# Window attention: the read-out R summed by 32x64 matmuls straight from the stored M, without spread copies

## The reference, cut to what matters

```
x = x + L0(gn(x))   # two GELU layers per pixel, 4 multipliers
x = x + L1(gn(x))   # 4x4 FIR filter
x = x + L2(gn(x))   # window attention
x = x + L3(gn(x))   # per-pixel 3x3 kernels, scatter-add, batch norm, leaky ReLU
```

```
q, k = split(x @ W_qk.T + b_qk)              # 4*64 query channels, 32 key channels
attn[c, d] = sum over the 64 pixels p of a window of q[c, p] * k[d, p]   # for each head
out = attn * temperature, laid out so that the 64 query channels c become the 64 pixels of the window
```

## Time and profile before

| what | us |
|---|---|
| median of 3 runs | 1149.85 |
| lowest, highest | 1148.54, 1150.21 |
| span of the profiled execution | 1148.0 |
| what lies around the span, if the profiled execution took the median | 1.85 |
| stage 4, first half of the images | 334.7 to 409.8 of the span |
| stage 4, second half | 832.2 to 906.4 |

### The profile page before, as it was taken

How to read it: one execution, slowest core, us unless ns; L and a number is a source line. 1 busy time by engine, 2 the same in 40 slices (tenths; PEclk the granted TensorE clock), 3 DMA queues, 4 the chain that set the end, 5 groups by cost and what they waited for, 6 DMA issues and landing times. The chain is left out here.

```text
span 1148.0 us, 22784 instructions
## 1 busy us (share of the span) xinstructions
PE 952.7 (83%) x6876; PEld 650.8 (57%) x6876; DVE 867.1 (76%) x1211; ACT 693.3 (60%) x860; POOL 317.6 (28%) x265
## 2 busy tenths in 40 slices
PE   5699977979989977845999949799999788676774
PEld 4333327968878875334433349688778683233332
DVE  7477788877757944876687878877769646799796
ACT  5799972323358853547999923234388563366564
POOL 0000009400026720510000066000077403466565
PEclk9799998989989988987999979989999898899897
DMA  9100000000000010233000000000000200024334
GB/s 294 37 0 0 0 0 1 0 1 1 0 1 1 0 73 5 69 114 107 0 0 0 0 1 1 1 1 0 1 1 0 74 0 1 0 86 135 106 114 146
DMA packets 51301, 39.32 MB, mean 34 GB/s; under 512 B 1600, under 2 KB 50880, under 8 KB 51008
## 3 DMA queue, kind: packets, MB, share of 16 engines
q1 hardware_dynamic: 51264, 38.85, 10.7%
HBM read 22.07 MB, written 16.78 MB: 34 GB/s over the span
## 5 line engine op out<-in xcount | busy, mean ns | idle before, releaser
L337 PE MATMUL ps<-work,cst 128*128 128x512 f32 x512 | 237.0, 610 | 17.5 <-ACT work L557 13.7
L337 PEld LDWEIGHTS ps<-work,cst 128*128 128x128 f32 x512 | 94.5, 193 | 158.8 <-issue 144.4
L256 PE MATMUL ps<-ST,work 128*128 x256 | 131.1, 635 | 9.7 <-DVE work L897 7.1
L557 ACT ACTIVATE work<-X,l0s 128x2048 f32 x64 | 136.6, 2140 | 2.6 <-SPq L294 2.6
L564 ACT ACTIVATE work<-ps 128x2048 f32<-128x2048 f32 x64 | 123.1, 1923 | 8.2 <-PE ps L337 8.0
L1019 POOL TENSOR_TENSOR work<-cst,ksum 128x512 f32<-128x512 f32 x64 | 66.2, 1055 | 203.2 <-SPq L294 174.4
L806 DVE TENSOR_TENSOR work<-ps,cst 64x512 f32<-64x512 f32 x128 | 88.2, 689 | 39.1 <-PE ps L404 37.3
L984 POOL TENSOR_TENSOR co<-mv,cst 128x1 f32<-128x1 f32 x8 | 1.5, 191 | 392.1 <-DVEq L246 302.4
L450 PE MATMUL ps<-work,cst 128*64 128x128 f32 x1024 | 103.6, 287 | 6.7 <-ACT work L621 6.7
L586 ACT ACTIVATE work<-ps 128x512 f32<-128x512 f32 x80 | 47.8, 598 | 100.5 <-PE ps L357 100.5
L450 PEld LDWEIGHTS ps<-work,cst 128*64 128x64 f32 x1024 | 88.4, 141 | 18.7 <-issue 9.9
(11 more groups left out here) (99 smaller groups left out, 1774.3 us busy)
## 6 DMA issues: line engine op xcount, KB each, us to landing
work<-x SPq DMA_DIRECT2D x32, 512.0 KB, 4.9
out<-work SPq DMA_DIRECT2D x64, 256.0 KB, 2.8
work<-choose SPq DMA_DIRECT2D x2, 2048.0 KB, 8.4
cst<-consts SPq DMA_DIRECT2D x1, 1009.5 KB, 9.6
cst<-consts SPq DMA_DIRECT2D x1, 64.0 KB, 2.0
```

Source lines behind the costliest of these rows:

```text
L256: return nc.tensor.matmul(ps[:, bank, :], sel[:, n, :], ST[:, ds(s * (4 * H), 4 * H)], start=True, stop=True)
L337: last = pe.matmul(ps[:, 4 * (m % 2) + b, :], wg[:, m, :], yb[:, m, b * BANK:(b + 1) * BANK], start=True, stop=True)
L557: act.activation(yb[:, m, :], X[:, ds(s * PIX + i * CHUNK, CHUNK)], ACT.Gelu, scale=l0s[:, m:m + 1], bias=l0s[:, MULTI + m:MULTI + m + 1]) ...
```

## The change: what it does

In stage 4, R is summed per pair of window rows (`DUOS` = 8 pairs). The tile `mh`, its spread copies and its memsets go. Each matmul takes the 32 partitions of one image straight from `mall` (moving, 128 columns with a stride) and from `wq` (64 weight columns), and writes the PSUM bank of its image: 4 row tiles (images, banks 0 to 3) x 2 column tiles. A pair has 4 heads x 2 x 4 = 32 matmuls, in an order in which eight different tiles follow each other. ACT copies the four banks by two activations of 128x1024 with a rearrangement to the order of the transposes, and PE transposes 16 blocks into banks 4 to 7, each bank after DVE has used its last contents. The products of the query bias are laid out by image row (`qb` as [2, 8, 8, 8] with the row j outside the window q), so that the adds on X run over 64 numbers in a row; DVE's first add becomes a `scalar_tensor_tensor`. The loops over `s` of PE, ACT and DVE, and stage 4's loops on these engines, are written out.

```diff
+DUOS = NWIN // 2
-        mh, _e = part(_e0, [RING, NWIN, G, C])
-        rs, _e = part(_e, [RING, 4, P])
-        qb, _ = part(_e, [RING, NWIN // 2, WS, WS])
+        rs, _e = part(_e0, [RING, NWIN, P])
+        qb, _ = part(_e, [RING, WS, NWIN // 2, WS])
...
-            with pe.Fori(0, NS) as s:
+            for s in range(NS):
...
+                def r_sum(i):
+                    nn = s * DUOS + i
+                    if nn:
+                        pe.wait_ge(s_rc, 2 * nn)
+                    for hd in range(HEADS):
+                        for hp in range(2):
+                            for g in range(G):
+                                rows = slice(C * g, C * g + C)
+                                m_in = mall[rows, 2 * i:2 * i + 2, hp::2, hd * CK:hd * CK + CK]
+                                o = ps[N * hp:N * hp + N, g, :].rearrange("p (m d) -> p m d", m=NWIN)
+                                last = pe.matmul(o[:, :, hd * CK:hd * CK + CK], wq[rows, hd, :],
+                                                 m_in.rearrange("p a b d -> p (a b) d"), start=True, stop=True)
+                    last.then_inc(s_r, 1)
+                def r_back(i):
+                    nn = s * DUOS + i
+                    pe.wait_ge(s_rc, 2 * nn + 2)
+                    for b in range(4):
+                        if nn:
+                            pe.wait_ge(s_x3, 4 * nn - 3 + b)
+                        for q in range(4):
+                            last = pe.transpose(ps[:, 4 + b, q * P:q * P + P], rs[:, i % RING, 4 * b + q, :], ident)
+                        last.then_inc(s_xt, 1)
+                r_sum(0)
+                for i in range(DUOS):
+                    if i + 1 < DUOS:
+                        r_sum(i + 1)
+                    r_back(i)
...
-            with act.Fori(0, NS) as s:
+            for s in range(NS):
...
+                for i in range(DUOS):
+                    nn = s * DUOS + i
+                    act.wait_ge(s_r, nn + 1)
+                    if nn >= RING:
+                        act.wait_ge(s_xt, 4 * (nn - RING) + 4)
+                    for g in range(0, G, 2):
+                        src = ps[:, g:g + 2, :].rearrange("p g (m d) -> p g m d", m=NWIN)
+                        dst = rs[:, i % RING, :, :].rearrange("p m (g d) -> p g m d", g=G)[:, g:g + 2, :, :]
+                        act.activation(dst, src, ACT.Copy).then_inc(s_rc, 1)
...
-                dve.memset(mh[:, 0, :, :, :], 0.0).then_inc(s_mz, 1)
-                dve.memset(mh[:, 1, :, :, :], 0.0).then_inc(s_mz, 1)
-                with dve.Fori(0, 16) as i:
+                for w1 in range(NWIN):
...
-                    dve.tensor_tensor(windows(0), windows(0), qb[:, 0, :, :, :].rearrange("p q j i -> p j q i"),
-                                      ALU.add).then_inc(s_xb, 1)
+                    dve.scalar_tensor_tensor(half_windows(0), half_windows(0), 1.0,
+                                             qb[:, 0, :, :, :].rearrange("p j q i -> p j (q i)"), ALU.mult, ALU.add
+                                             ).then_inc(s_xb, 1)
-                        src = ps[:, 2 + hf, :].rearrange("p (q j i) -> p j q i", j=WS, i=WS)
+                        src = ps[:, 4 + 2 * (w1 % 2) + hf, :].rearrange("p (q j i) -> p j q i", j=WS, i=WS)
...
                         pool.tensor_tensor(
-                            qb[:, hf, :, :, :].rearrange("p q j i -> p q (j i)"),
-                            c("bq").rearrange("p (o n) -> p o n", o=1).broadcast_to([P, half, N]),
-                            ksum[:, ds(w1 * NWIN + hf * half, half)].rearrange("p (q o) -> p q o", o=1
-                                                                               ).broadcast_to([P, half, N]),
+                            qb[:, hf, :, :, :],
+                            c("bq").rearrange("p (j o i) -> p j o i", o=1, i=WS).broadcast_to([P, WS, half, WS]),
+                            ksum[:, ds(w1 * NWIN + hf * half, half)].rearrange("p (o q e) -> p o q e", o=1, e=1
+                                                                               ).broadcast_to([P, WS, half, WS]),
                             ALU.mult).then_inc(s_qb, 1)
-                    v = X3[:, ds(s * W + w1 * WS, WS), half * WS:2 * half * WS].rearrange("p j (q i) -> p j q i", i=WS)
-                    pool.tensor_tensor(v, v, qb[:, 1, :, :, :].rearrange("p q j i -> p j q i"), ALU.add
+                    v = X3[:, ds(s * W + w1 * WS, WS), half * WS:2 * half * WS]
+                    pool.tensor_tensor(v, v, qb[:, 1, :, :, :].rearrange("p j q i -> p j (q i)"), ALU.add
```

More of the change, by code:

```diff
@@ L194, in build @@
         s_zero = sem("keys_buffers_zeroed")
-        s_mz = sem("m_buffer_zeroed")
         s_pt = sem("patches_transposed")
@@ L209, in build @@
         s_xg = rsem("query_bias_added_second", "pool", 1)
-        s_mh = sem("mh_ready")
         s_r = sem("r_summed")
-        s_rc = rsem("r_copied", "act")
-        s_xt = rsem("r_transposed", "pe")
-        s_x3 = rsem("x3_written", "dve")
+        s_rc = sem("r_copied")
+        s_xt = sem("r_transposed")
+        s_x3 = sem("x3_written")
         s_xc = sem("x3n_ready")
@@ L313, in _ @@
             pe.sem_inc(s_in, 2 * RING)
-            pe.sem_inc(s_r, 2 * RING)
             pe.wait_ge(s_ident, 16)
-            with pe.Fori(0, NS) as s:
+            for s in range(NS):
                 with pe.Fori(0, W // LW // LOADS) as i:
@@ L438, in _ @@
                 stage_end(pe, s, 3)
[L441 to L451, removed]
-                    last.then_inc(s_r, 1)
@@ L695, in _ @@
             start_rings(dve, "dve")
-            with dve.Fori(0, NS) as s:
+            for s in range(NS):
                 def measure(i, u):
@@ L826, in _ @@
                 stage_end(dve, s, 3)
-                dve.memset(mh[:, 1, :, :, :], 0.0).then_inc(s_mz, 1)
-                with dve.Fori(0, 16) as i:
+                for w1 in range(NWIN):
                     def half_windows(hf):
-                        return X3[:, ds(s * W + i * WS, WS), 64 * hf:64 * hf + 64]
+                        return X3[:, ds(s * W + w1 * WS, WS), 64 * hf:64 * hf + 64]
                     def measure_x3(hf):
-                        dve.wait_ge(s_x3, after(s * NB + i * 2 + hf))
+                        dve.wait_ge(s_x3, s * NB + w1 * 2 + hf + 1)
                         alone(dve)
-                        dve.bn_stats(stats[:, ds(i * 12 + 6 * hf, 6)], half_windows(hf))
+                        dve.bn_stats(stats[:, 12 * w1 + 6 * hf:12 * w1 + 6 * hf + 6], half_windows(hf))
                     def windows(hf):
                         return half_windows(hf).rearrange("p j (q i) -> p j q i", i=WS)
-                    dve.wait_ge(s_qb, s * NB + i * 2 + 1)
-                    dve.tensor_tensor(windows(0), windows(0), qb[:, 0, :, :, :].rearrange("p q j i -> p j q i"),
-                                      ALU.add).then_inc(s_xb, 1)
+                    dve.wait_ge(s_qb, s * NB + w1 * 2 + 1)
+                    dve.scalar_tensor_tensor(half_windows(0), half_windows(0), 1.0,
+                                             qb[:, 0, :, :, :].rearrange("p j q i -> p j (q i)"), ALU.mult, ALU.add
+                                             ).then_inc(s_xb, 1)
                     for hf in range(2):
-                        nn = s * NB + i * 2 + hf
-                        dve.wait_ge(s_xt, after(nn))
-                        dve.wait_ge(s_xg if hf else s_xb, after(s * NWIN + i, 1))
-                        src = ps[:, 2 + hf, :].rearrange("p (q j i) -> p j q i", j=WS, i=WS)
+                        dve.wait_ge(s_xt, s * NB + w1 * 2 + hf + 1)
+                        dve.wait_ge(s_xg if hf else s_xb, after(s * NWIN + w1, 1))
+                        src = ps[:, 4 + 2 * (w1 % 2) + hf, :].rearrange("p (q j i) -> p j q i", j=WS, i=WS)
                         dve.tensor_tensor(windows(hf), windows(hf), src, ALU.add).then_inc(s_x3, 1)
```

1 line of the change is left out of this document (removed).

## The result

The changed kernel takes 1116.69 us (median of 4 runs, 1116.11 to 1117.37) against 1150.03 for the kernel before on the same chip: a ratio of 0.971, 95% interval 0.970 to 0.972. That is 33.3 us less. The forecast was 1130.3 with a range of 1126 to 1143, so the sign held, and the gain was undersized by 13.6 us. The profiled span is 1115.4 (1148.0 before).

What follows compares the result with a forecast made beforehand. No engine was full; PE's cycle of 4.20 us and POOL's with DVE of 4.27 bound stage 4. 14.6 + 1.7 + 3.3 = 19.6 off the span of 1148.0, plus 1.85 around it, gave 1130.3, range 1126 to 1143.

Steps and rivals of the forecast that it cites:

- The new cycle: Stage 4's window row: DVE's first add goes ahead of POOL's, 3.82 us a row in place of 4.27, 14.6 saved.
- 1.6 to 1.8 was to show that I was right: Sign for the forecast, late in stage 4: POOL's add at about 1.6 to 1.8 us, DVE's at 0.7.
- that rival: Stage 4: POOL's add keeps going first, 4.28 us a row, 7.4 less in all, 1142.4 us; 15%.
- two cycles of nearly the same length: Stage 4 before the change: PE's cycle of 4.20 us a window row and POOL's of 4.27, closed with DVE.
- PE and ACT: Stage 4, per pair: PE 4 us, ACT's loop 4.2, both under the 7.6 of DVE and POOL, so off the path.
- Start of the stage: Start of stage 4, up to DVE's first add on PSUM: 1.4 us less in the first half, 0.3 in the second.
- Between the halves: Turn between the halves: without PE's branch back DVE goes on at about 499.1, 3.3 us less.
- The price of the longer code: PE's written-out stage 4, some 1,300 instructions: taken as 0, at most one more stall of 3.4 us in each half.
- The unrolling brings nothing or costs fetches: Rival on the written-out loops: 1133.6 us with no gain, 1140 with a stall in each half; 8%.
- That tiles don't overlap: Rival in stage 4: PE is the bound, 9.4 us a pair, 1156.7 us, deciding from 0.08 us a record; 5%.

Runs made afterwards that it cites:

- A: The changed kernel itself, against the kernel before: 1116.69 us, ratio 0.971.
- experiment 4: A with the bias products in the old window order and a plain tensor_tensor on DVE: 1130.22 us, ratio 0.983.
- experiment 3: A with the loops over the halves put back on PE, ACT and DVE: 1130.22 us, ratio 0.982.
- experiment 1: The kernel before with only the loops over the halves written out on PE, ACT and DVE: 1137.22 us, ratio 0.989.
- experiment 8: A with the four heads of a tile one after another in the same 32 matmuls: 1147.58 us, ratio 1.000.
- experiment 10: A with POOL's output add held back until DVE has read row n+3 out of PSUM: 1096.84 us, ratio 0.954.
- experiment 5: experiment 4 with POOL's add also made to wait until DVE's first add is done: 1127.89 us, ratio 0.981.
- experiment 7: The kernel before with R's sums over heads 0 and 1 alone, half of the terms left out: 1138.83 us, ratio 0.990.

## Why the prediction was wrong, step by step

- **The new cycle (3.82 us): the size right, partly by luck.** Measured 3.81, with POOL's product at 1.10 (1.05 to 1.10 said), DVE's only wait for POOL, and POOL's add 1.12 behind DVE's, as said. But I closed the row over DVE: 0.22 from POOL's add to DVE's next, and 0.66 for L844. Measured are 0.10 (360.24 against 360.14) and 0.77, which cancel. By DVE's own path, with a first add of 0.67, a row would be 3.70, and one row of A is (343.11 to 346.81); the other 0.1 is POOL's product, behind which DVE's first add waits. POOL's add takes 1.46, where 1.6 to 1.8 was to show that I was right. From the first L820 (337.45) to the end of the last L806 (396.66) it is 59.2 us; 59.4 were said. The tie that settles the order was decided by 0.06 us, with the outcome reversed in experiment 4. The 15% for that rival was fair. My reading of two cycles of nearly the same length before hid that PE's 4.20 set every row.
- **PE and ACT: right.** `r_sum` 1.26 for 64 records, just under the 1.3 to 2.0 said, each copy 1.02 (1.04 said). Both off the path.
- **Start of the stage: undersized.** I took a value between the full and the half clock for the second `r_sum` and let DVE start 7.2 us in. In A the granted clock stays at 1.00 there, and DVE starts after 5.2, in the second half 5.4: 3.3 and 2.0 less than before where 1.4 and 0.3 were said, 3.6 of the 4.3 between 16.3 and 20.6. Part of this is luck: with the same matmuls and the clock at 0.50 experiment 3 has 6.6. No run shows what decides it.
- **Between the halves: the step that failed.** "3.3 less" and "The price of the longer code ... I take 0" took the loop over the halves to cost only its jump. The jump was sized rightly (idle 3.91 to 0.50). But writing the loop out is worth 12.8 us (experiment 1), 13.5 when taken back (experiment 3). Of this 3.7 to 4.3 are at the turn; the rest, some 9 us, is the term that the sum put at nothing. In the table for A it is the 7.6 of the other stages. What the loop does inside the stages is seen in one place: with it put back, DVE starts 0.22 after POOL's add and not 0.10 (358.35 against 358.13 in experiment 3), as it did before. In that very stage it buys 0.01 a row, since POOL's product sets the row there. That the rest of the gain is the sum of many such steps is argued, not shown: where it arises stays open, for no run put the loop back for one stage alone, and single stages moved by up to 1.6 us between kernels with the same code in them.
- **The rivals.** "The unrolling brings nothing or costs fetches" fell: in A's stage 4 PE is never idle for "issue", and the longest such gap of its weight loads, 2.3 us, leaves DVE waiting for POOL alone. That tiles don't overlap was no danger in the order as written, and real in another one: 0.072 us a record (experiment 8), under the 0.08 that the prediction named as the point from which it decides. That point was worked out for a row at the full clock, and there it held (late rows 3.81); the loss came at the start, which it left out.

The sum with what was measured: 20.6 + 4.3 + 7.6 is 32.5 of the profiled spans' 32.6. Against the 19.6 forecast, 7.6 are the other stages, 3.6 the starts of stage 4 and 1.0 the turn.

## What to carry to other kernels

Where two engines meet at something they share, look which one starts first, by how much, and who has slack; if the one without slack comes second, hold the other back a little, by a slightly longer operation or by a wait for what stands just ahead of the first one's instruction (experiment 10); a wait for the end of that instruction gives part of the gain away (experiment 5). And look at every loop with the same pair, not only the one that is being changed. Count a loop written out at more than its jump: here it was worth over three times the jump, and where the rest lies has to be measured. Small matmuls on tiles overlap only if neighbours in the program lie on different tiles.

## What was not expected of the hardware

- A cycle of VectorE and GpSimd has two stable forms of the same instructions: 4.27 (experiment 4) or 3.83 us (experiment 7) in stage 4, 2.07 or 1.68 in the output loop. 0.03 to 0.06 us at one row choose between them. The Trainium skill (SBUF - State Buffer, Who interferes with whom) says that issue order decides who blocks; the traces agree (DVE 0.77 or 1.77), and show that the first order perpetuates itself.
- An instruction that queues behind the other's work starts more cheaply than one that is released by its end: POOL's add ends 1.12 us after DVE's when it is queued (A) and 1.48 after it when released by its end (experiment 5), 3.81 us a row against 4.07, though POOL's own product is shorter in the latter.
- 64 records of 32x64 tiles, neighbours on different tiles, lie 0.016 us apart, on one tile 0.072, at the full clock; full-width ones 0.113.
- With the same matmuls at the start of stage 4 the granted clock was 1.00 in A and 0.50 in experiment 3, and the start 5.2 or 6.6 us long.
